# Every third expert tile of an attention and mixture-of-experts layer: gathered as quarter rows and turned in 32x32 blocks by VectorE instead of by TensorE

## What is computed

```python
xn = _layernorm(x)
x = x + attention(xn, Wq, Wk, Wv, Wo) + ffn(xn, gate_w, expert_w, expert_b)

def ffn(x, gate_w, expert_w, expert_b):      # 4096 tokens, 512 features, 8 experts
    xf = x.reshape(B * S, D)
    top_vals, top_idx = jax.lax.top_k(xf @ gate_w.T, 2)
    w = jax.nn.softmax(top_vals, axis=-1)
    y_all = jnp.einsum('td,eod->teo', xf, expert_w) + expert_b[None, :, :]
    y_sel = jnp.take_along_axis(y_all, top_idx[:, :, None], axis=1)
    return jnp.sum(y_sel * w[:, :, None], axis=1)
```

## Time and profile before

| | |
|---|---|
| runs of the kernel before | 985.04, 986.21, 988.06 us, median 986.21 |
| profiled execution | 989.46 us, its span 987.7 us |
| TensorE busy | 919.4 us, 93% of the span |
| VectorE busy | 739.2 us, 75% |
| GpSimd busy | 561.2 us, 57% |
| ScalarE busy | 437.1 us, 44% |
| DMA | 188.63 MB, 191 GB/s on the mean |

### The profile page before, as it was taken

The page is one execution under the profiler, slowest core; times in us unless marked ns, Lnnn a source line. Parts: engine busy times, 40 slices in busy tenths (PEclk is TensorE's granted clock), DMA queues, the critical chain, the costliest instruction groups (busy, mean ns, idle before and its releaser), DMA issues.

```text
span 987.7 us, 18755 instructions
## 1 busy us (share of the span) xinstructions
PE 919.4 (93%) x6589; PEld 450.7 (46%) x6589; DVE 739.2 (75%) x1327; ACT 437.1 (44%) x711; POOL 561.2 (57%) x553
## 2 busy tenths in 40 slices
PE   2899898899899999989999999998999999999887
PEld 1344344344354544545555555553444444444333
DVE  7888988798789899954444444467788888788865
ACT  5267867757755443431111221133434454334432
POOL 1545677575675446663333333238877888778741
PEclk9999999999999999999999999999999999999999
DMA  6365678598677443396655555455555564555431
GB/s 242 107 225 183 192 268 312 170 331 288 193 261 287 138 163 127 115 335 193 204 175 176 176 177 171 161 193 171 184 176 182 186 196 140 156 184 175 162 109 54
DMA packets 107963, 188.63 MB, mean 191 GB/s; under 512 B 11872, under 2 KB 65248, under 8 KB 102624
## 3 DMA queue, kind: packets, MB, share of 16 engines
q1 hardware_dynamic: 97072, 152.03, 44.4%
q0 software_dynamic: 10800, 35.40, 12.7%
HBM read 117.13 MB, written 70.25 MB: 190 GB/s over the span
## 4 chain that ended last, share of the span: by engine, by line
PE 65%; DVE 14%; DMA 7%; POOL 5%; ACT 4%; issue 3%; SPq 1%; DVEq 0%; ACTq 0%; POOLq 0%
PE psum L952 19%; PE psum L1037 10%; PE psum L1061 6%; PE psum L1000 5%; PE psum L987 5%; PE psum L1003 4%; PE psum L969 4%; PE psum L1046 4%; PE psum L929 4%; DVE top L1486 4%; DMA c_rows<-c_turn 2%; DMA sum_sb<-x 2%; PE psum L971 2%; ACT pT L764 1%; DMA x_blk<-xn_rows 1%
## 5 line engine op out<-in xcount | busy, mean ns | idle before, releaser
L764 ACT ACTIVATE pT<-psum,factors 128x512 f32<-128x512 f32 (+1 forms) x352 | 218.2, 642 | 247.2 <-PE psum L987 238.2
L1486 DVE TENSOR_REDUCE top<-psum 128x1 f32<-128x384 f32 (+3 forms) x352 | 209.9, 634 | 20.8 <-PE psum L971 19.9
L1037 PE MATMUL psum<-xT,w_att 128*128 128x512 f16 x768 | 196.5, 381 | 6.9 <-DVE xT L1437 4.7
L952 PE MATMUL psum<-w_exp,x_gT 128*128 x852 | 195.3, 379 | 0.6 <-DVE x_gT L1442 0.6
L610 POOL DMA_INDIRECT x_g<-xn_rows,tok_of x71 | 67.3, 948 | 131.8 <-PE psum L929 129.5
L969 PE MATMUL psum<-k_stack,q_stack 96*128 96x384 f16 (+3 forms) x512 | 126.6, 300 | 14.3 <-DVE top L1486 13.2
L987 PE MATMUL psum<-q_stack,k_stack 98*128 98x256 f16 (+3 forms) x512 | 128.4, 303 | 7.4 <-ACT pT L764 4.5
L1442 DVE TENSOR_TENSOR x_gT<-psum,x_gT 128x512 f16<-128x512 f32 x71 | 49.0, 692 | 104.4 <-ACT x_gT L788 85.5
L952 PEld LDWEIGHTS psum<-w_exp,x_gT 128*128 128x128 f16 x852 | 83.3, 98 | 85.6 <-issue 0.9
L788 ACT ACTIVATE x_gT<-psum 128x512 f16<-128x512 f32 x71 | 42.3, 597 | 170.0 <-PE psum L929 167.5
L600 POOL TENSOR_TENSOR o_hl<-o_sb,o_hl 128x512 f16<-128x512 f32 x31 | 36.5, 1177 | 129.9 <-ACT o_hl L778 128.7
(11 more groups left out here) (175 smaller groups left out, 1296.3 us busy)
## 6 DMA issues: line engine op xcount, KB each, us to landing
y_rows<-y_sb SPq DMA_DIRECT2D x71, 256.0 KB
w_in<-w_all SPq DMA_DIRECT2D x12, 1024.0 KB, 11.4
q_stack<-qk_rows SPq DMA_DIRECT2D x96, 128.0 KB
k_stack<-qk_rows SPq DMA_DIRECT2D x96, 128.0 KB
x_in<-x SPq DMA_DIRECT2D x8, 1024.0 KB, 9.5
qk_rows<-q_hl SPq DMA_DIRECT2D x32, 256.0 KB
qk_rows<-k_hl SPq DMA_DIRECT2D x32, 256.0 KB
xn_rows<-x_in SPq DMA_DIRECT2D x8, 1024.0 KB, 5.1
```

The lines of the kernel that those rows point to most:

```text
L764: act.activation(p_of(j, h, heads), banks[BANK_T + (NT_ * n + k) % 2][:, 0:W], ACT.Exp, scale=factors[:, 0:1]).then_inc(exp_done, 1)
L952: now = pe.matmul(banks[s % 4], x_gT[s % 4][:, xp * C + c, :], w_exp[:, bass.ds(e, 1), wp, c, :].rearrange("p e d -> p (e d)"), start=n == ...
L1037: now = pe.matmul(bank, w_att[:, what, wp, c, g * P:(g + 1) * P], xT[b % 2][:, xp * C + c, :], start=at_pass == 0, stop=at_pass == 3 * C - 1)
L1486: return dve.tensor_reduce(out=top[:, h:h + heads, i], in_=banks[BANK_S + k % 2][:, 0:heads * W].rearrange("p (h t) -> p h t", h=heads), a ...
```

## The change

For the 22 tiles 5, 8, ..., 68 (`BLK`) the way from memory to `x_gT` is another one:

- GpSimd issues four indirect DMAs per tile instead of one, each of 128 quarter rows (128 fp32, 512 bytes). The quarter t of the tile's buffer takes tokens 32 t to 32 t + 31; partition p fetches quarter p // 32 of token 32 t + p % 32. The indices stand in `tok_blk`.
- VectorE transposes all 32x32 blocks of the buffer in place (`turn_xg_blocks`). After it the partition is a feature, the column a token. It walks the buffer with a step of 4 elements.
- ScalarE and VectorE read the halves from `x_g`, in place of PSUM, with a step of 4 elements.
- TensorE has no turn for these tiles.

The features of a chunk are now those with f % 4 = c, in all tiles, so the expert weights are stored in that order, and in the other 49 tiles TensorE's four transposes read `x_g` with a step of 4 elements. Once per run `tok_blk` is made: a copy of the identity four times over (`four16`, GpSimd), an fp16 copy of the token numbers (`tok16`, VectorE), four small matmuls (`spread_tokens`), and one VectorE operation (`block_tokens`).

```diff
+    FIRST_BLK = 5
+    BLK = list(range(FIRST_BLK, NTILE, 3))
...
+    xn_quarters = xn_rows.rearrange("t (a f) -> (t a) f", f=P)
...
+    four16 = at("four16", [P, P // HD, C, HD], F16, logit_at)
+
+    tok_blk = small_sb[:, 0:P // HD * len(BLK)].bitcast(I32).rearrange("p (t s) -> p t s", t=P // HD)
...
+    def rows_till(s):
+        return s + 1 - blks_till(s)
+
+    def blks_till(s):
+        return len([i for i in BLK if i <= s])
+
+    def got(s):
+        return sum(64 if i in BLK else 16 for i in range(s % 4, s + 1, 4))
...
+    def by_chunks(part):
+        return part.rearrange("p c (t r) -> p c t r", r=HD)
+
+
+    def of_blocks(rows):
+        return rows.rearrange("p (t r c) -> p c t r", c=C, r=HD)
...
             def gather_x(s):
                 u = s % 4
-                if s >= 4:
-                    pool.wait_ge(xg_turned, s - 3)
+                if s - 4 in BLK:
+                    pool.wait_ge(xg_lo, s - 3)
+                elif s >= 4:
+                    pool.wait_ge(xg_turned, rows_till(s - 4))
                 elif s < 2:
                     pool.wait_ge(sum_stored[s], 16 * (EARLY // 2))
                 else:
                     pool.wait_ge(qk_lo, rope_no(2 * (N1 + 3) - 1))
-                pool.indirect_dma_start(x_g[u][:], None, xn_rows, bass.IndirectOffsetOnAxis(ap=tok_of[:, s:s + 1], axis=0))\
-                    .then_inc(gathered[u], 16)
+                if s in BLK:
+                    if s == FIRST_BLK:
+                        pool.wait_ge(blk_done, 1)
+                    i = BLK.index(s)
+                    for t in range(P // HD):
+                        pool.indirect_dma_start(x_g[u][:, t * P:(t + 1) * P], None, xn_quarters,
+                                                bass.IndirectOffsetOnAxis(ap=tok_blk[:, t, i:i + 1], axis=0)).then_inc(gathered[u], 16)
+                else:
+                    pool.indirect_dma_start(x_g[u][:], None, xn_rows, bass.IndirectOffsetOnAxis(ap=tok_of[:, s:s + 1], axis=0))\
+                        .then_inc(gathered[u], 16)
...
+                if n == CHOOSE + 2:
+                    pool.wait_ge(chosen_done, 1)
+                    pool.tensor_copy(four16[:], ident16[:].rearrange("p (t r) -> p t r", r=HD).unsqueeze(2).broadcast_to([P, P // HD, C, HD]))\
+                        .then_inc(four_made, 1)
...
             def high_xg(s):
-                act.wait_ge(xg_turned, s + 1)
+                if s in BLK:
+                    act.wait_ge(xg_blocked, blks_till(s))
+                else:
+                    act.wait_ge(xg_turned, rows_till(s))
                 if s >= 4:
                     act.wait_ge(y_done, s - 3)
                 elif s < 2:
                     act.wait_ge(qk_roped, rope_no(2 * (N1 + 2) + s))
                 else:
                     act.wait_ge(pv_done, J * N1)
-                act.activation(x_gT[s % 4][:, 0:C, :].rearrange("p c t -> p (c t)"), banks[BANK_QV + s % 4], ACT.Copy).then_inc(xg_hi, 1)
+                if s in BLK:
+                    act.activation(by_chunks(x_gT[s % 4][:, 0:C, :]), of_blocks(x_g[s % 4][:]), ACT.Copy).then_inc(xg_hi, 1)
+                else:
+                    act.activation(x_gT[s % 4][:, 0:C, :].rearrange("p c t -> p (c t)"), banks[BANK_QV + s % 4], ACT.Copy).then_inc(xg_hi, 1)
...
+            def spread_tokens():
+                pe.wait_ge(four_made, 1)
+                pe.wait_ge(tok16_done, 1)
+                for t in range(P // HD):
+                    now = pe.matmul(banks[BANK_T + 1][:, t * len(BLK):(t + 1) * len(BLK)],
+                                    four16[:, t, :, :].rearrange("p a r -> p (a r)"),
+                                    tok16[:, FIRST_BLK:NTILE:3], start=True, stop=True)
+                now.then_inc(blk_spread, 1)
...
             def turn_xg(s):
-                pe.wait_ge(gathered[s % 4], 16 * (s // 4 + 1))
+                pe.wait_ge(gathered[s % 4], got(s))
                 if s >= 4:
                     pe.wait_ge(xg_lo, s - 3)
                 elif s == 0:
@@ -939,13 +997,18 @@
                     pe.wait_ge(sum_done, EARLY)
                 else:
                     pe.wait_ge(o_read, N1)
-                turn_tile(x_g[s % 4][:], BANK_QV + s % 4).then_inc(xg_turned, 1)
+                rows = x_g[s % 4][:].rearrange("p (f c) -> p c f", c=C)
+                for k in range(C):
+                    now = pe.transpose(banks[BANK_QV + s % 4][:, k * P:(k + 1) * P], rows[:, k], ident32[:])
+                now.then_inc(xg_turned, 1)
...
+                elif s == BANK_T + 1:
+                    pe.wait_ge(blk_done, 1)
...
+            spread_tokens()
             for s in range(NTILE):
-                if 0 < s < NTILE - 1:
+                if 0 < s < NTILE - 1 and s + 1 not in BLK:
                     turn_xg(s + 1)
                 expert(s)
...
             def low_xg(s):
                 dve.wait_ge(xg_hi, s + 1)
                 hi, lo = (x_gT[s % 4][:, h * C:(h + 1) * C, :].rearrange("p c t -> p (c t)") for h in range(2))
-                dve.tensor_tensor(lo, banks[BANK_QV + s % 4], hi, ALU.subtract).then_inc(xg_lo, 1)
+                if s in BLK:
+                    hi, lo = (by_chunks(x_gT[s % 4][:, h * C:(h + 1) * C, :]) for h in range(2))
+                    dve.tensor_tensor(lo, of_blocks(x_g[s % 4][:]), hi, ALU.subtract).then_inc(xg_lo, 1)
+                else:
+                    dve.tensor_tensor(lo, banks[BANK_QV + s % 4], hi, ALU.subtract).then_inc(xg_lo, 1)
+
+            def turn_xg_blocks(s):
+                dve.wait_ge(gathered[s % 4], got(s))
+                here = x_g[s % 4][:].rearrange("p (t r c) -> p t c r", c=C, r=HD)
+                dve.transpose(here, here).then_inc(xg_blocked, 1)
+
+            def block_tokens():
+                dve.wait_ge(blk_spread, 1)
+                dve.tensor_scalar(tok_blk.rearrange("p t s -> p (t s)"), banks[BANK_T + 1][:, 0:P // HD * len(BLK)], float(D // P), quarter,
+                                  ALU.mult, ALU.add).then_inc(blk_done, 1)
 
             def read_tokens():
                 dve.wait_ge(tok_summed, 1)
+                dve.tensor_copy(tok16[:], banks[BANK_QV][:, 0:NTILE]).then_inc(tok16_done, 1)
...
+            block_tokens()
             low_xg(2)
             for s in range(NTILE):
+                if s + 4 in BLK:
+                    turn_xg_blocks(s + 4)
                 if s + 3 < NTILE:
...
+    def by_strided_features(w):
+        return w.T.reshape(P, C, w.shape[0])
+
+    mats = [by_strided_features(a["L0_ffn_expert_w"][e]) for e in range(E)]
```

10 lines of the change are left out of this document (8 added, 2 removed).

## The result

The changed kernel takes 992.90 us (median of 4 runs, 991.80 to 995.17) against 986.41 (985.04 to 988.06): a ratio of 1.0066, 95% interval [1.0047, 1.0085]. It is slower by 6.5 us where 8.4 us less were forecast. Its profiled execution took 991.8 us, span 990.0.

What follows compares the result with a forecast made beforehand. TensorE, without a gap in the expert stage, was taken as the bound. Terms -9.6 + 0.8 + 0.1 + 0.3 = -8.4 gave 977.8 us against the median 986.21; range 975.8 to 992.5.

Steps and rivals of the forecast that it cites:

- Removed, -9.6: Expert stage: 22 tiles lose their TensorE transposes, 0.44 us each, -9.6 us if nothing else becomes the bound.
- VectorE, 0: Added block transposes, 0.70 to 1.4 us each, and strided halves fit VectorE's and ScalarE's idle time: cost 0.
- The other 49 tiles, +0.3: TensorE transposes reading x_g at a step of 4 fp32: strided weight loads cost +0.3 us, ends 0 and 15.4.
- the two small bounds: Strided weight loads in 47 turns: 0 at the lower end, 1.6 us if a 0.06 us load doubles to 0.12.
- the 0.06 us between two load starts: First turn after an idle stretch, 434.02 to 434.08: read as a contiguous weight load releasing its port after about 0.06 us.
- The main rival: Transposes of the 47 row tiles: strided weight loads cost +15.4 us and eat the gain, 992.9 us; chance 0.17.
- Once-only work, +0.1 (0 to 0.5): Ahead of the stage: four small matmuls, tok16 copy and tok_blk arithmetic, +0.1 us together; four16 copy covered by slack.
- GpSimd and the start, +0.8 (0 to 1.7): Quarter gathers keep pace at 1.26 us each; at the stage's start tile 8's late quarters cost TensorE +0.8 us.
- The slack of 1.07 us: Between the end of x_gT's low half and the expert matmuls reading it, where the turn between is gone: 1.07 us spare.

Runs made afterwards that it cites:

- one_gather: Changed kernel with each block tile fetched by one row gather instead of four quarter gathers (values not the reference's): 982.51 us, ratio 0.9948.
- strided_only: Kernel before, with all 71 TensorE turns reading x_g at a step of 4 fp32 and expert weights stored in that order: 990.46 us, ratio 1.0030.
- prep_only: Kernel before plus the changed kernel's once-only preparation, unused; one gather per tile, all turns on TensorE: 992.29 us, ratio 1.0054.
- quarters_only: Kernel before with the four quarter gathers and their index table for 22 tiles; TensorE turns every tile (values not the reference's): 1001.18 us, ratio 1.0146.
- dummies: Kernel before with three unread gathers added ahead of every third tile's own gather, 66 in all: 997.97 us, ratio 1.0121.
- the other pair: two_ahead without and with 64 bytes of padding behind tok16, on different chips: ratio 1.0002 without, 0.9943 with.
- two_ahead: Changed kernel with first block tile 11 instead of 5, and TensorE turning tile s+2 ahead of expert s from tile 4 on: 987.49 us, ratio 1.0002.
- two_quarters: Changed kernel with two quarter gathers per block tile instead of four (values not the reference's): 982.69 us, ratio 0.9961.
- halves_evenly: Kernel before with two half-row gathers instead of one whole-row gather for each of 71 tiles (values not the reference's): 996.03 us, ratio 1.0101.
- two_ahead_4th: Changed kernel with block tiles 11, 15, ..., 67 and TensorE turning two tiles ahead from tile 4 on: 987.39 us, ratio 1.0007.
- busy_66: Kernel before with nine plain GpSimd additions, about 3.5 us, ahead of the gather of each of tiles 5, 8, ..., 68: 988.83 us, ratio 1.0011.

## Why the prediction was wrong, step by step

**Removed, -9.6.** Right. one_gather's stage is 8.1 us shorter; with the turns' 2.0 that is 10.1.

**VectorE, 0.** Right in its own terms: 1.14 us, between the ends of 0.70 and 1.4, and free wherever its data was there (one_gather). It is also where late quarters reach TensorE, as at 449.04.

**The other 49 tiles, +0.3.** The mechanism was right, the term mis-sized: 2.9 us for 69 turns (strided_only), so 2.0 for 47, near the upper of the two small bounds (1.6) and far from 15.4. I took the lower side of a range whose only direct row, the 0.06 us between two load starts, gave 1.6 when doubled. What the Trainium skill says of a different line for each access ("Advanced Engine Details and Errata", section Memory Cachelines) holds here in direction, at 0.011 us per transpose. The main rival's price, 992.9, is the measured time to the tenth. That is luck, and its cause is refuted: the turns cost 2.0 us, not 15.4.

**Once-only work, +0.1 (0 to 0.5).** Wrong: 5.3 us in prep_only, and in the changed kernel 2.5 of the 6.5 us lie outside the 4.0 that its stage is longer. The term counted instructions and waits and not that new tensors move all that is allotted behind them. 192 bytes made the large buffers start off a multiple of 256: 3.0 us by the padding of the changed kernel, 5.8 in the other pair, both across chips.

**GpSimd and the start, +0.8 (0 to 1.7).** This is the step that failed. It read: "It holds, with 1.1 us to spare per three tiles; from 1.44 us per gather on, GpSimd sets the pace." The rate was right, gathers start 1.25 us apart, and GpSimd does pause. But the step priced a queue and looked only at when data lands. What the runs show in its place: behind four and more gathers in a row TensorE's semaphore updates arrive late, in the changed kernel by up to 1.3 us in most triples and by 4.2 us behind the twelve at the start. ScalarE, GpSimd's next gather and, over the low half, TensorE wait for them. Together with the quarters of tile 5 this is 12.1 us, over half of it (6.3) in the first 26 us of the stage. The late quarters themselves cost 1.8 us, about what was counted (1.7), but at tile 5 and not at tile 8. The slack of 1.07 us that the prediction found behind the low half is less than the delay, so 0.2 to 0.3 us remain each time. Where the slack is 1.51 us (quarters_only, dummies) next to nothing does, and two_ahead, with three microseconds more, has few gaps.

The account: -9.6 + 2.0 + 12.1 + 3.0 = +7.5, measured +6.5. The last term comes from another chip; the two profiled executions, 989.46 and 991.8 us, don't show it, since that of the kernel before lies 3 us above its median.

**What is settled and what is open.** Shown: the loss in the stage is the extra gathers' (one_gather against the changed kernel; quarters_only; dummies, where they touch nothing); it has a threshold between four and six per three tiles (two_quarters); most of it falls at the start of the stage, and what a late update costs after that depends on the slack behind the turn (halves_evenly, two_ahead, two_ahead_4th). Argued only: that the length of a run is what counts. Four chips' traces agree with it, those of one chip show runs of six and more without it. Why an update of TensorE should wait for GpSimd's gathers, and whether the chip is the reason where it doesn't, stays open, and so does what busy_66 was to tell. Argued in part: that the start off a multiple of 256 bytes is the time outside the stage; the later landings are shown to be its doing.

## What to carry to other kernels

Work put on an engine with time to spare can still cost its neighbours: before a single gather is split into several, look at how many follow one another and at what TensorE's semaphores release just then, and give that release a tile of slack. Look first at the start of a stage, where the queue is behind: most of the loss fell there. A new small tensor is not free either: check what its size does to the start address of every buffer that is allotted behind it. And when a rival's price matches the result, test its mechanism all the same.

## What was not expected of the hardware

- High halves start 0.64 us behind a turn in the kernel before. Where the turn falls late in a run of gathers they mostly start 1.4 to 2.5 us behind it on four of five chips, and up to 5.0 us in two_ahead.
- 192 bytes of shift, from a multiple of 256 to 192 beyond one: w_rows lands in 8.7 us in place of 7.5, x_blk in 5.3 in place of 4.9, and in 7.6 and 4.8 with the padding.
- A step of four fp32: VectorE's transpose of 128x512 takes 1.14 us (0.70 contiguous), ScalarE's conversion 1.11 (0.60), VectorE's subtraction 1.07 (0.69); TensorE's transposes follow each other 0.042 / 4 = 0.011 us later.
